# Softmax denominators from VectorE sums of the probability blocks, block-turned reciprocals, and a preparation moved into the up pass

## The reference

```python
s = SCALE * log(k_length)[:, None, None, None]
attn = einsum('bhdq,bhdk->bhqk', heads(layernorm(x)), heads(ctx))
out  = einsum('bhqk,bhdk->bhdq', softmax(s * attn, axis=-1), heads(ctx))
x = x + out
h = layernorm(x)
x = x + moe(h)      # softmax gate, top 2 of 8 experts with a capacity, each with a low-rank branch,
                    # plus 0.2 * (gelu(h @ sw1 + sb1) @ sw2 + sb2 + gelu(h @ swd) @ swu) for every row
```

## Time and profile before

| | |
|---|---|
| median of 3 runs | 1451.3 us (1448.96 to 1455.62) |
| the profiled execution | 1449.71 us |
| its span, first to last instruction | 1446.6 us |
| attention, shared layer and routing | about 0 to 690 us |
| the eight experts | about 690 to 1446 us |
| windows 1 to 6, from one `rank` to the next | 77.9 us each in the steady part, 148 to 537 us |

### The profile page before, as it was taken

How to read it: one execution, slowest core, us unless ns; L and a number is a source line. 1 busy time by engine, 2 the same in 40 slices (tenths; PEclk the granted TensorE clock), 3 DMA queues, 4 the chain that set the end, 5 groups by cost and what they waited for, 6 DMA issues and landing times.

```text
span 1446.6 us, 28003 instructions
## 1 busy us (share of the span) xinstructions
PE 1380.2 (95%) x11731; PEld 993.1 (69%) x11796; DVE 775.3 (54%) x1281; ACT 716.0 (49%) x1072; POOL 233.6 (16%) x219
## 2 busy tenths in 40 slices
PE   5788999999999999999999999999999999999995
PEld 1252736464554647375788889998888888888884
DVE  6885757575665757454643625536254362552620
ACT  4765665657565656564434435345343443443411
POOL 4820000000000000443100303012030030300202
PEclk9999999999999999999999999999999999999998
DMA  8513131312213032116532625426254262531402
GB/s 281 173 52 88 44 96 52 87 46 81 59 60 88 30 102 89 23 24 217 163 106 77 177 90 154 132 98 158 90 155 125 80 180 90 151 105 65 96 1 37
DMA packets 93215, 145.46 MB, mean 101 GB/s; under 512 B 15529, under 2 KB 36153, under 8 KB 93090
## 3 DMA queue, kind: packets, MB, share of 16 engines
q1 hardware_dynamic: 80802, 118.47, 25.2%
q0 software_dynamic: 12288, 25.21, 9.3%
HBM read 109.47 MB, written 34.15 MB: 99 GB/s over the span
## 4 chain that ended last, share of the span: by engine, by line
PE 89%; DVE 5%; issue 2%; ACT 2%; DMA 1%; POOL 0%; POOLq 0%; SPq 0%; DVEq 0%; ACTq 0%
PE banks L1642 24%; PE banks L1667 24%; PE banks L1547 11%; PE banks L1565 10%; PE banks L1494 7%; PE banks L1442 3%; PE banks L1474 3%; PE banks L1604 1%; PE banks L1682 1%; DVE rowmax L1122 1%; PE banks L1521 1%; PE banks L1533 1%; DVE rden L1139 1%; DMA split_parts<-hidden 1%; ACT hidden L917 1%
## 5 line engine op out<-in xcount | busy, mean ns | idle before, releaser
L1667 PE MATMUL banks<-hidden,w2h 128*128 128x0 bf16 x2048 | 324.6, 276 | 0.0
L917 ACT ACTIVATE hidden<-banks,scales 128x512 f32<-128x512 f32 x256 | 171.4, 687 | 139.1 <-PE banks L1474 95.8
L1667 PEld LDWEIGHTS banks<-hidden,w2h 128*128 128x128 bf16 x2048 | 198.2, 98 | 29.3
L1122 DVE TENSOR_REDUCE rowmax<-banks 128x1 f32<-128x512 f32 x256 | 173.6, 685 | 71.3 <-PE banks L1442 70.9
L1667 PE MATMUL banks<-hidden,w2l 128*128 128x0 bf16 x1024 | 198.6, 276 | 0.0
L1010 ACT ACTIVATE hf<-banks,b1cols 128x640 f32<-128x640 f32 x128 | 101.7, 795 | 179.0 <-PE banks L1642 178.1
L1565 PE MATMUL banks<-w2h,hidden 128*128 128x512 bf16 x498 | 179.6, 379 | 1.3 <-issue 1.2
L1258 DVE TENSOR_TENSOR w1l<-stage,w1h 128x2048 bf16<-128x2048 f32 x32 | 73.4, 2293 | 198.7 <-ACT w1h L984 198.7
L1642 PE MATMUL banks<-eth,w1h 128*128 128x0 bf16 x1024 | 136.0, 276 | 0.0
L1642 PE MATMUL banks<-eth,w1l 128*128 128x0 bf16 x1024 | 135.9, 276 | 0.0
L1642 PE MATMUL banks<-etl,w1h 128*128 128x0 bf16 x1024 | 135.9, 276 | 0.0
(11 more groups left out here) (182 smaller groups left out, 2007.7 us busy)
## 6 DMA issues: line engine op xcount, KB each, us to landing
stage<-in_L_ffn_w SPq DMA_DIRECT2D x64, 1024.0 KB, 5.3
split_parts<-hidden SPq DMA_DIRECT2D x16, 512.0 KB, 3.4
QS<-split_parts SPq DMA_DIRECT2D x48, 128.0 KB, 2.5
KS<-split_parts SPq DMA_DIRECT2D x48, 128.0 KB, 2.8
xin<-in_x SPq DMA_DIRECT2D x16, 256.0 KB, 3.1
cin<-in_ctx SPq DMA_DIRECT2D x16, 256.0 KB, 2.8
out_rows<-xin SPq DMA_DIRECT2D x16, 256.0 KB, 2.0
normed_rows<-x2r SPq DMA_DIRECT2D x16, 256.0 KB, 2.0
```

What stands on the lines that cost most here:

```text
L917: ac.activation(prob[n % NPH], bank(score_bank[unit]), ACT.Exp, scale=scales[:, g // 2:g // 2 + 1]).then_inc(s_exp, 1)
L1122: dv.reduce_max(rowmax[g % 2][:, i:i + 1], bank(score_bank[unit]), X_AXIS).then_inc(s_max, 1)
L1667: issued = mm(half_of(bank(b0 + j)).shape_from_register(bank_cols(e, j)), w[:, fb, rows], half_of(a[:, fb, :], j).shape_from_register(slot ...
```

## The change

- For groups 2 to 15, `values` has k = 1 only. VectorE adds the probabilities of the four key blocks instead: a new unit `sum` (g, t, j) adds two heads at a time, 128 x 1024 f32, six per group (t = 1 adds blocks 0 and 1, t = 2 and 3 add to the result), in the tile `prob_sum`, which is the memory of `late_stage`. The sums are placed from i = 6 to i = 14, the last at the start of the next stage. A new unit `ones` then makes the denominators with four f32 matmuls per group, at i = 3 of the second half (group a) and n = 2 of the up pass (group b). `exp` waits for the sum that last read its buffer.
- `den` has three steps for all groups: a transpose of 32 x 32 blocks from PSUM, a reciprocal of one column of each block (128 x 16), and a transpose of that result, repeated 32 times, back. `average` has five steps instead of six.
- For groups 2 to 15 the cast in `x_hi` moves from VectorE to ScalarE (new semaphores s_norm, s_xhi). For all groups the cast in `gate` moves from VectorE to ScalarE (s_xth).
- In windows 1 to 6 only `prepare(b + 2)` stays in the first half. `prepare(a + 4)` runs in the up pass before, one step per n from n = 3; with it its POOL step and its SP transfers.
- `side` starts at i = 5 of the first half (windows 1 to 7) and i = 3 of the second, before at 0 and 2.

```diff
     def value_step(g, t):
-        for k in range(2):
+        for k in range(2) if g < 2 else (1,):
             add("values", g, t, k)
 
     def average(g):
-        for q in range(QT):
-            add("den", g, q)
+        for k in range(3):
+            add("den", g, k)
             yield
...
                 side = left_over[:]
                 if not last:
-                    side += [prepare(g + 2), prepare(g + 3)]
+                    side += [prepare(g + 3)] if w else [prepare(g + 2), prepare(g + 3)]
...
             for i in range(UNITS):
+                if w and i % 2 and i > GH:
+                    sums.append((g * UNITS + i, (g, i // GH, i % GH // 2)))
                 add("exp", g, i)
...
-                if i >= 2 * k:
+                if i >= (ONES if k else 5 if w else 0):
                     one_of(side, 1 if k == 0 and w and i < LATE else 2)
...
+                ready_sums(g * UNITS + i - 1)
                 one_of(downs, 2 if k == 0 and i < 2 else 1)
                 if i % GH == 2 and (i > GH or k == 1):
                     value_step(*divmod(g * QT + i // GH - 1, QT))
+                if w and k == 1 and i == ONES:
+                    add("ones", g - 1)
...
+        ahead = prepare(a + 4) if a + 4 < GROUPS else iter(())
         for n, _ in enumerate(shared_up(w)):
             next(score, None)
+            if n >= PREP:
+                next(ahead, None)
+            if n == 0:
+                ready_sums(b * UNITS + UNITS)
             if n == 1:
                 value_step(b, QT - 1)
+            if w and n == ONES - 1:
+                add("ones", b)
...
+                    if g >= 2:
+                        act.wait_ge(s_norm, g - 1)
+                        ac.activation(split[g % 2][:, 0, :], xn[:, :], ACT.Copy).then_inc(s_xhi, 1)
...
+                    if n >= 2 * UNITS + NPH:
+                        was_g, was_i = divmod(n - NPH, UNITS)
+                        act.wait_ge(s_sum, sum_no(was_g, was_i // GH, was_i % GH // 2))
                     ac.activation(prob[n % NPH], bank(score_bank[unit]), ACT.Exp,
                                   scale=scales[:, g // 2:g // 2 + 1]).then_inc(s_exp, 1)
...
+                elif kind == "gate":
...
+                    ac.activation(xth[p % 2][:, :, col:col + P], x2t[:, :, :], ACT.Copy).then_inc(s_xth, 1)
...
+                elif kind == "sum":
+                    _, g, t, j = unit
+                    pairs = slice(2 * j * L, 2 * j * L + 2 * L)
+                    dve.wait_ge(s_exp, g * UNITS + t * GH + 2 * j + 2)
...
+                    dv.tensor_tensor(prob_sum[:, pairs], prob_pairs[j] if t == 1 else prob_sum[:, pairs],
+                                     prob_pairs[t % 2 * 2 + j], ALU.add).then_inc(s_sum, 1)
                 elif kind == "den":
...
+                        if g >= 2:
+                            dve.wait_ge(s_ones, g - 1)
...
-                    dv.reciprocal(rden[:, cols], bank(3 if g % 2 else 5)[:, cols]).then_inc(s_den, 1)
+                        dv.transpose(rden[:, :], bank(3 if g % 2 else 5)).then_inc(s_den, 1)
+                    elif k == 1:
+                        dve.wait_ge(s_den, g + 1)
+                        link(dv.reciprocal(rblock[:, :], by_block[:, :, 0]))
+                    else:
+                        dve.wait_ge(s_dve, chain)
+                        link(dv.transpose(rden[:, :], rblock[:, :].unsqueeze(2).to_broadcast([P, L // HD, HD])))
...
-                    link(dv.tensor_copy(xth[p % 2][:, :, col:col + P], x2t[:, :, :]))
-                    mark_xt = chain
...
+                elif kind == "ones":
+                    g = unit[1]
+                    pe.wait_ge(s_sum, sum_no(g, QT - 1, 1))
+                    for h in range(GH):
+                        issued = mm(bank(3 if g % 2 else 5)[HD * h:HD * h + HD, :], ones_f[:, :], prob_sum[:, h * L:h * L + L],
+                                    start=True, stop=True)
+                    issued.then_inc(s_ones, 1)
```

87 lines of the change are left out of this document (58 added, 29 removed).

## The result

The changed kernel takes 1426.65 us, the median of four runs (1425.55 to 1430.85), against 1452.15 us for the kernel before beside it; the ratio is 0.983, with a 95% interval of 0.980 to 0.986. The profiled execution took 1425.8 us with a span of 1423.9 us, which is 22.7 us less than the span before. Around the span lie 1.9 us, where it was 3.1 before. On another chip the same two kernels gave 1430.71 and 1449.77 us, a ratio of 0.985 (0.982 to 0.988).

The account below looks back on a forecast made before the run. The prediction took PE as the bound. Steady windows -23.0, window 1 -3.0, window 7 -2.0 and last up pass +0.3 gave -27.7 us from 1449.7, then 1.6 us to the median: 1423.6 us, range 1413 to 1441.

Parts of the forecast that it names:

- PE is last, and a block is worth 0.89 us: Steady windows: PE bounds; each ones part removed saves 0.89 us, each `ones` unit costs 1.07, 5.0 us gained per window.
- Prices on VectorE: New VectorE instructions: sum 1.22 us, transpose 0.69, 16-column reciprocal 0.23; VectorE 58.9 us and ScalarE 50.2 per steady window.
- First half: the ScalarE wait stays: End of the first half: PE's 0.43 us wait for a ScalarE exponential stays about as it is.
- Second half: 15.5 us of VectorE in PE's 15.3, allowance 0.4 us: Second half: VectorE's needed work about even with PE's; 0.4 us a window allowed for this and for `xt_lo`.
- the prediction's faster rival: Whole kernel: all 35 us arrive, 1414 us, supported by overlap between VectorE instructions that the stretch left uncounted; chance 0.14.
- Up pass: +0.2 us: Steady up pass: PE gains 0.89 us from a block and pays 1.07 for `ones`; nothing else charged.
- Window 0 and up pass 0: nothing: Window 0 and up pass 0: cheaper reciprocals and a moved cast against the 2.9 us preparation; called 0.
- Window 1: -3.0 us: Window 1: first half -1.8 us, second half -1.2 with VectorE taking PE's place; -3.0 us together.
- Window 7: Window 7: routing starts 7.5 us later, `place` comes at 593.3, one iteration before the half's end; window -2.0 us.
- PE busy 35 us less: Profile after: PE's busy time lower by about 35 us, from 5.0 us per window or 34.9 us for 14 groups.
- The total: Whole kernel: -27.7 us summed over windows, giving 1423.6 us; chance of the forecast 0.56.
- the no-gain case: Whole kernel: sums cost in waits what PE gains, for example by stopping beside GpSimd work; 1451 us, chance 0.04.

Follow-up runs that it names:

- prep_back: Changed kernel with both preparations back in the first half, as before the change; 1433.37 us, ratio 0.987 to the kernel before.
- few_sums: Changed kernel with four of the six sums per group cut to 8 of 1024 columns; 1420.17 us, ratio 0.979 to the kernel before.
- long_sums: Changed kernel with a second VectorE instruction of 512 columns behind each sum, result unchanged; 1470.38 us, ratio 1.007 to the kernel before.
- double_sums: Changed kernel with a second VectorE instruction of 1024 columns behind each sum; 1509.18 us in one run.
- turned_only: Kernel before with only the turned reciprocals (two transposes, one 16-column reciprocal, three steps for four); 1460.8 us, one run, kernel before 1460.87 on that chip.
- gate_later: Changed kernel with one empty step behind the residual of each odd group; 1444.48 us, one run on a slower chip, steady window 73.41 us.
- rows_later: Changed kernel with the two rows2 steps of group 0 moved from the end of window 0 into window 1's first half; 1422.66 us, one run.
- all_three: Changed kernel with the empty step, group 0's rows2 in window 1, and window 7's routing steps from i = 2; 1417.12 us, ratio 0.977 to the kernel before.

## Why the prediction was right, and where it was not

- **PE is last, and a block is worth 0.89 us.** Right: 0.87 us per block, `ones` 1.09 and 1.14 us for 1.07. These terms make 0.3 us a window of the miss. 22 blocks and units of ones are left of 64 (8 and 14), as said.
- **Prices on VectorE.** Right: sum 1.22 us, transposes 0.71 for 0.69, reciprocal 0.25 for 0.23. Busy in a steady window 57.7 us for 58.9, ScalarE 49.5 for 50.2.
- **First half: the ScalarE wait stays.** Right: 0.55 us for 0.43. prep_back shows what the moved preparation is worth, 1.16 us, and that it is ScalarE's.
- **Second half: 15.5 us of VectorE in PE's 15.3, allowance 0.4 us.** The step failed on the safe side. The stretch from the first transpose to the end of the maximum that the last score needs (280.58 to 294.97) took 14.4 us, and ended 0.6 us before that score (295.55). The difference to 15.5 is a count: the prediction had `rows2` and the copy of the gate logits ahead of that maximum, 1.3 us, and they stand behind it. The durations of the 20 instructions add up to 14.3 us. Ten of them start before the one ahead has ended in the record (a sum starts at 284.84 and the maximum behind it at 285.98, 1.14 us for a duration of 1.22; a maximum steps by 0.60 for 0.68), which gives back 0.8 us, as the prediction's faster rival had it; but 0.9 us of gaps, 0.7 of them two waits, take it up again. few_sums shows that nothing was paid; the room of 0.3 us a sum is the estimate from long_sums and double_sums.
- **Up pass: +0.2 us.** The step missed 0.36 us, the largest single part of the steady miss: a list with a step less moves what follows it in the plan. The prediction took `den` with three steps for a saving alone. turned_only and gate_later show it from both sides.
- **Window 0 and up pass 0: nothing.** Window 0 was right, up pass 0 was not: +1.95 us, of which 1.6 us lie where the clock is lower, behind a wait that grew from 1.6 to 3.4 us. The work in the pass, which the step was about, costs 0.4 us (rows_later).
- **Window 1: -3.0 us.** Measured -1.5 us, and on the other chip +0.3. The first half gave 2.6 us for 1.8, the second lost 1.15 where 1.2 were to be gained. The term named VectorE as last. few_sums takes 5.6 us of VectorE's work out of this stretch (busy 25.6 us in place of 31.2) and shortens it by 0.7 us only, at the same granted clock (0.88 in both), so the amount of VectorE's work isn't the cause. Its place in the queue may be: few_sums leaves whole the two sums that exponentials wait for, and they wait for sums 3.8 us in both. What the rows show as new is these exponentials behind sums and the lower clock, 0.77 in place of 0.93 in the second half; ScalarE's wait at the end of the first half was there before. In the changed kernel's second run the clock of the stretch is 0.83 and it takes 44.74 us. How the loss divides is not settled.
- **Window 7.** Right to 0.4 us in length and to 0.3 us in the place of its matmul in the first run; in the second it took 77.43 us, 1.0 less than before. PE's wait at `place` grew from 1.7 to 2.9 us.
- **PE busy 35 us less.** Measured 23.9 us. The prediction took 5.0 us from each of seven windows. The stretches at the lower clock count here too, and a steady window has 4.04 us less of it (76.72 by the earlier trace rows to 72.68), as its length says.
- **The total.** It is near because the misses are small and partly cancel: the allowance of 0.4 us a window was not paid, while the gate's 0.36 us and up pass 0 were not foreseen. That the time missed by 3.1 us and the span by 5.0 is luck: 1.2 us are the shorter time around the span, the rest is the spread between a profiled run and the median.
- **GpSimd beside VectorE.** All 84 sums took 1.21 to 1.23 us, among them the 13 that lie beside one of GpSimd's small steps (128 x 1), so the no-gain case had no ground:

```profile
L1195 DVE TENSOR_TENSOR late_stage<-late_stage,hidden x16: 1214/1220/1227, 194.4 to 299.8; 128x1024 f32<-128x1024 f32 x16
```

In these 13 places the sum starts first, and it is GpSimd's step, 0.16 us behind it, that becomes longer: 1.46 to 1.49 us, where it takes 0.55 alone. The `norm` that waits for it starts without a gap on VectorE in the steady windows, so nothing was paid for that either.

Against that, the subtraction L1241 with two inputs in SBUF took 1.52 us at 76.08, beside GpSimd's subtraction of weight parts (74.61 to 79.73), where 0.69 is its steady time. The rule of the Trainium skill (SBUF — State Buffer, Who interferes with whom), that a VectorE instruction with two SBUF inputs is held up by a GpSimd instruction that reads SBUF, agrees with this row; it cost time in the first 80 us of the kernel. Beside the sums, which start first, it was GpSimd's step that became longer.

## What to carry over

When work leaves the engine that is last, look at each place where it already waits for another: the wait takes up the gain, and on PE a longer wait can also lower the clock behind it, so that the gain turns into a loss of the same size. When a list of interleaved steps gets shorter or longer, compare the order of everything behind it in the plan, unit by unit; an empty step can be worth more than a cheaper instruction. And to say which engine ends a stretch last, count what stands ahead of the instruction that is needed, unit by unit: here a count was off by 1.3 us, more than the overlap between instructions and the waits, 0.8 and 0.9 us.

## What the runs showed of the hardware

- The same wait of PE, in the same kernel, is followed by different granted clocks from run to run: 3.4 and 3.5 us before `rank`, then 0.76 and 0.52 from 78 to 85 us; 2.9 us at `place`, then 1.00 and 0.89. Single waits of 1.6 us (before) and 1.0 us (rows_later, all_three) ahead of `rank` were followed by 1.00.
- A transpose of 32 x 32 blocks over 128 x 512 f32 costs 0.71 us, the price of an addition of that size (0.69), also when its input is one column repeated 32 times.
- On one chip the kernel before took 1460.9 us, in place of 1450 to 1454, and PE stood still for up to 9.1 us at a time in the last up pass of gate_later with no releaser in the profile. Its cause is open; only the steady windows of those four runs were used for more than a rough time.
